# Banded attention inside a four-block kernel: strips loaded straight into the query and key tiles, the first group of heads loaded one stage early, four head groups folded by one product

## The chip, the cores and the metric

The kernel runs on one core of a Trainium2 chip. The metric is the device time of one execution in microseconds (us); lower is better. Engines are named as in the profile: PE is TensorE's matmul row and PEld its weight-load row, DVE is VectorE, ACT is ScalarE, POOL is GpSimd, SP is SyncE, which here only issues transfers. A name with a q behind it (SPq, ACTq, POOLq) is the queue that feeds the engine.

## The reference, cut to what matters

The input is x of shape (8, 512, 128): eight sequences of 512 tokens and 128 features. It passes through an expert layer, a state-space layer, the same expert layer, a routed expert layer ("ffn1"), banded attention, and the routed expert layer again. The change is in the attention and in the end of the ffn1 ahead of it.

```python
# attention: 16 heads of d = 8 features, blocks of C = 64 queries, a band 64 wide
qkv = (x @ Wqkv.T + bqkv).reshape(B, S, 3, H, d).transpose(2, 0, 3, 1, 4)
q, k, v = qkv[0], qkv[1], qkv[2]            # k and v padded by 32 on both sides
scores = einsum('bhncd,bhnld->bhncl', qc, kb) / sqrt(d)
scores = where(band, scores, -inf)          # band = (j >= c) & (j < c + 64)
o = einsum('bhncl,bhnld->bhncd', softmax(scores), vb)
out = o.transpose(0, 2, 1, 3).reshape(B, S, D) @ Wout.T + bout
```

## The kernel before

The program is a row of blocks, each with its own instruction list for every engine, and a barrier of all five engines between two of them: `front` (everything up to the first ffn1), `ffn1` with tag `_f` (in the profile: `_f1` in instruction lists), `attention` (tiles end in `_a`), and `ffn1` again with tag `_f1b`. `attention` is a generator: before its own block it hands out helpers (`opening`), with which the ffn1 block ahead prepares sequence 0, so that queries, keys and values are computed while the last expert tiles are still worked on.

**How attention is tiled.** A block is 32 queries against 96 keys (`QB`, `KW`), so a sequence has `NB` = 16 blocks. A group is 4 heads (`HG`), and a sequence has 4 groups, numbered n = 4s + g over the whole stage. A unit u is half of the blocks of one group (8 blocks); there are 8 units to a sequence and 64 in all. For one block one product gives the scores of all four heads of the group: the stationary operand is a block-diagonal query tile `qd` of 128 rows (head, copy, feature) by 128 columns (head, query), the moving operand 96 columns of the key tile `kT`. Queries and keys are split into a rounded part (`q_hi`, `k_hi`) and its rest (`q_lo`, `k_lo`), and the four copies of a head's 8 features are the four pairings of these parts.

**The way of a query.** ACT writes `q_hi`, DVE `q_lo`, both [128 features, 512 tokens]. SP stores each twice to `q_rows` in DRAM (`store_queries`), the same for keys (`store_keys`; for sequence 0 ACT issues these). `strips` reads a group's 128 rows back as `k_strips` and `q_strips` (256 KB each, two transfers per group). Then DVE copies the key strip into `kT` (`set_keys`, L1296) and ACT makes four copies of 32 rows each into the diagonal of `qd` (`set_queries`, L1287). There are three `qd`/`kT` pairs (`RQ`) and two strip pairs.

**The loop.** Step t of the PE loop is: scores of unit t+2 (L1311, 8 products), transposes of unit t's probabilities (`turn`, L1337, 8), the products with the values of unit t-1 (`weigh`, L1356, 8 products of two passes), and `gather` of unit t-2 (L1378, 8 products of two passes). `PLACES` adds, in the first four steps of a sequence, the next sequence's transposes, queries, keys and values and the last one's output projection (`project_pe`, L1265). The other engines follow in the same order: DVE masks and takes the maximum (L1320, L1325), POOL subtracts it (L1217), ACT takes the exponential (L1329), PE turns, ACT copies (L1344), PE weighs, DVE normalizes (L1363, L1367), POOL keeps each row's own head (`keep_own`, L1224).

**The fold.** After `weigh` a block's output has 128 rows (head, query) by 32 columns. `gather` multiplies it, as the stationary operand of 32 columns, with `fold` [128, 32], which sums the four quarters, and puts the result in rows 32g to 32g+31 of the bank `BZ`: one product for each block and each group. `BZ` is cleared once by DVE. When the eighth unit is in, ACT copies `BZ` to `oT` (`project_act`).

**Start of the stage.** After the barrier SP waits for the stores of sequence 0, loads groups 0 and 1 and stores and reloads the values. POOL clears the borders of all `kT` and all `qd` (L1228 to L1232), takes the norm of sequence 1 (`norm_root`), clears parts of the value tiles, adds the bias (L1212) and only then comes to the first subtraction. ACT's order is: queries 0, queries 1, exponential of unit 0, `norm_out(1)` (L104), exponential of unit 1. PE's third score product waits for group 1's tiles, and its next work after that is the transposes of sequence 1 (L114).

**End of the ffn1 ahead.** Its last part is a loop over J from 24 to 33 (`EJ` to `AJ`+1, `AJ` = 32), in which PE multiplies up (J) and down (J-2), with the opening's four pieces at J = 30, 31, 32, 33. POOL adds eight tiles of routed rows (L1679), and after the second it takes the norm of sequence 0, which waits for DVE's statistics (L74).

Of the kernel before, what the change touches and what calls it, by code (L numbers as in the profile page):

```python
# [984 lines left out]
def attention(nc, S, C, bank, K, a):  # L985
# [11 lines left out]
    with ExitStack() as ctx:  # L997
# [138 lines left out]

        def prep_act(eng, s, name):
# [6 lines left out]
            elif name in ("q", "k"):  # L1144
# [20 lines left out]
        yield dict(load_weights=load_weights, store_queries=store_queries, store_keys=store_keys, set_ones=set_ones, set_masks=set_masks, biases_pe=biases_pe, biases_dve=biases_dve,  # L1165
                   norm_stats=norm_stats, norm_root=norm_root, norm_out=norm_out, prep_pe=prep_pe, prep_act=prep_act, prep_dve=prep_dve)

        qd = [sb(f"qd{r}", [P, NB, HG, QB], F32R) for r in range(RQ)]
        kT = [sb(f"kT{r}", [P, PADDED], F32R) for r in range(RQ)]
        q_strips, k_strips = two("q_strips", [P, SEQ]), two("k_strips", [P, SEQ])  # L1170
# [4 lines left out]
        o1, oT = two("o1", [P, UB, GD]), sb("oT", [P, SEQ])  # L1175

        def strips(eng, s, g):
            n, heads = s * HG + g, slice(HG * g, HG * g + HG)
            if n >= 2:
                eng.wait_ge(q_set.sem, q_set.at(n - 2))  # L1180
                eng.wait_ge(k_set.sem, k_set.at(n - 2))
            eng.dma_start(k_strips[n % 2][:], k_rows[s, heads].rearrange("r c d t -> (r c d) t")).then_inc(strip_in[n % 2].sem, 16)
            eng.dma_start(q_strips[n % 2][:], q_rows[s, heads].rearrange("r c d t -> (r c d) t")).then_inc(strip_in[n % 2].sem, 16)
# [934 lines left out]
```

## Time and profile before

| | |
|---|---|
| median of 3 runs | 1942.12 us (1941.42 to 1945.63) |
| profiled execution, its own time | 1944.77 us |
| its span in the profile | 1943.0 us |
| mean granted PE clock | 0.966 of full speed |
| PE / PEld busy | 1770.6 us (91%) / 1520.2 us (78%) |
| DVE / ACT / POOL busy | 1223.9 / 1210.5 / 1200.7 us (62 to 63%) |
| ffn1 block ahead: first instruction after its barrier | 1142.0 us |
| attention block: released at / ends at | 1380.0 us / 1707.7 us |
| second ffn1 block ends | 1943.0 us |

The profile is one execution; times in it count from its span's start. Busy time of PE comes from modelled ends of matmuls, so the distance between starts of successive groups tells more than the length of one.

### The profile page before, as it was taken

What the parts mean: (1) busy time and instruction counts of PE and PEld (TensorE: products, weight loads), DVE (VectorE), ACT (ScalarE), POOL (GpSimd) and SP (SyncE); (2) the same over time, 40 slices, a digit from 0 to 9 for tenths busy, and PEclk for the clock granted to TensorE, in tenths of its full rate; (3) what the DMA queues carried; (4) which work ended last, traced back from release to release, by engine and by line L of the source; (5) the groups of instructions that cost most, each with busy time, mean ns of one, the idle gap of its engine ahead of it and who ended that gap; (6) DMA issues with size and microseconds to landing.
All of it is one profiled execution on the core that took longest, in us unless ns stands there. A gap on an engine that the chain in (4) does not pass through costs nothing. (4 is left out here: it accounts for less than half of the span.)

```text
span 1943.0 us, 35709 instructions
## 1 busy us (share of the span) xinstructions
PE 1770.6 (91%) x12117; PEld 1520.2 (78%) x12117; DVE 1223.9 (63%) x2897; ACT 1210.5 (62%) x2022; POOL 1200.7 (62%) x1195
## 2 busy tenths in 40 slices
PE   7999998999989989888789989999699999989998
PEld 6878776777777778766567878888599999978876
DVE  2358876767787677777886446433467666646433
ACT  3567777787687877778775554333477767543442
POOL 3148776776767757778896725465556555534664
PEclk9999998999999999999989989999799999989999
DMA  5023323222223323322231401112454444101113
GB/s 143 1 85 117 98 90 103 90 90 93 90 88 102 103 78 106 91 83 84 83 95 44 134 13 43 38 46 66 145 156 134 120 145 142 40 22 36 46 44 107
DMA packets 120638, 166.95 MB, mean 86 GB/s; under 512 B 13878, under 2 KB 55820, under 8 KB 120460
## 3 DMA queue, kind: packets, MB, share of 16 engines
q1 hardware_dynamic: 112716, 147.74, 25.3%
q0 software_dynamic: 7168, 15.87, 2.7%
q8 instruction: 101, 1.65, 0.3%
q10 hardware_dynamic: 576, 1.05, 0.2%
q14 instruction: 77, 0.63, 0.1%
HBM read 114.28 MB, written 50.33 MB: 85 GB/s over the span
## 5 line engine op out<-in xcount | busy, mean ns | idle before, releaser
L756 POOL TENSOR_TENSOR db<-du_m,bt 128x512 f32<-128x512 f32 x256 | 328.8, 1286 | 170.9 <-DVE bank L761 170.6
L761 DVE TENSOR_TENSOR_SCAN bank<-bank,db 128x512 f32<-128x512 f32 x256 | 312.6, 1221 | 27.2 <-ACT bank L746 27.0
L787 POOL TENSOR_TENSOR y_m<-y_m,ph 128x512 f32<-128x512 f32 x240 | 307.4, 1281 | 0.4 <-DVE ph L776 0.4
L746 ACT ACTIVATE bank<-dt_m,a_neg 128x512 f32<-128x512 f32 x256 | 176.2, 688 | 84.4 <-DVE ph L776 76.1
L776 DVE TENSOR_TENSOR ph<-bank,ct 128x512 f32<-128x512 f32 x240 | 165.9, 691 | 12.4 <-POOL y_m L787 4.4
L1217 POOL TENSOR_TENSOR s_a<-s_a,mx_a 128x768 f32<-128x768 f32 x64 | 94.1, 1470 | 89.1 <-DVE mx_a L1325 89.0
L1356 PE MATMUL bank<-vb_a,pT_a 96*128 96x64 f32 x1024 | 121.9, 272 | 0.2 <-DVE o_a L1367 0.2
L1356 PEld LDWEIGHTS bank<-vb_a,pT_a 96*128 96x128 f32 x1024 | 119.8, 192 | 0.3 <-DVE o_a L1367 0.3
L354 PEld LDWEIGHTS bank<-dn,hf2b 128*128 128x128 f32 x680 | 91.5, 196 | 14.3 <-DVE x_all L413 4.9
L354 PEld LDWEIGHTS bank<-dn,hf0b 128*128 128x128 f32 x688 | 91.5, 194 | 10.4 <-DVE x_all L413 2.8
L354 PEld LDWEIGHTS bank<-dn,hf1b 128*128 128x128 f32 x680 | 92.5, 198 | 8.1
L354 PEld LDWEIGHTS bank<-dn,hf2a 128*128 128x128 f32 x680 | 90.9, 195 | 8.5 <-DVE x_all L413 1.0
L354 PE MATMUL bank<-dn,hf2b 128*128 128x128 f32 x680 | 92.4, 280 | 5.5 <-DVE x_all L413 4.0
L354 PEld LDWEIGHTS bank<-dn,hf0a 128*128 128x128 f32 x688 | 90.5, 192 | 7.8 <-DVE x_all L413 0.3
L354 PEld LDWEIGHTS bank<-dn,hf1a 128*128 128x128 f32 x680 | 89.4, 192 | 7.5
L354 PE MATMUL bank<-dn,hf0b 128*128 128x128 f32 x688 | 92.2, 278 | 1.9 <-DVE x_all L413 1.9
L354 PE MATMUL bank<-dn,hf1b 128*128 128x128 f32 x680 | 92.8, 281 | 0.0
L354 PE MATMUL bank<-dn,hf2a 128*128 128x128 f32 x680 | 91.4, 278 | 0.5 <-DVE x_all L413 0.5
L354 PE MATMUL bank<-dn,hf0a 128*128 128x128 f32 x688 | 91.0, 275 | 0.0
L354 PE MATMUL bank<-dn,hf1a 128*128 128x128 f32 x680 | 89.8, 275 | 0.0
L1344 ACT COPY pT_a<-bank 96x512 f32<-96x512 f32 x128 | 68.1, 580 | 34.4 <-PE bank L1337 34.3
L1287 ACT CAST qd_a<-q_strips_a 32x512 fp32r<-32x512 f32 x128 | 78.7, 615 | 13.7 <-DMA q_strips_a<-q_rows 12.3
(453 smaller groups left out, 4952.0 us busy)
## 6 DMA issues: line engine op xcount, KB each, us to landing
bt<-bc_rows SPq DMA_DIRECT2D x128, 256.0 KB, 3.5
ct<-bc_rows SPq DMA_DIRECT2D x128, 256.0 KB, 3.4
sorted<-zero_row SPq DMA_DIRECT2D x64, 288.0 KB, 4.0
k_strips_a<-k_rows SPq DMA_DIRECT2D x32, 256.0 KB, 3.2
q_strips_a<-q_rows SPq DMA_DIRECT2D x32, 256.0 KB, 3.7
q_rows<-q_hi_a SPq DMA_DIRECT2D x16, 256.0 KB, 3.0
q_rows<-q_lo_a SPq DMA_DIRECT2D x16, 256.0 KB, 3.4
vb_a<-v_rows SPq DMA_DIRECT2D x16, 240.0 KB, 3.7
```

Of the source, the lines that this page charges most:

```text
L354: x = eng.matmul(Y.psum[:, t], hf[r][:, t], W["dn"][:, e, c, :], start=c == 0 and k == 0, stop=c == HC - 1 and k == NT - 1, skip_group_che ...
L746: eng.activation(DH[J % 2][:], dt[s % 2][:, j % NH, :], ACT.Exp, scale=a_neg[:, j % NH, j // NH:j // NH + 1]).then_inc(da_done.sem)
L756: eng.tensor_tensor(db[J % RD][:], du[s % 2][:, j % NH, :], bt[N % RB][:], ALU.mult).then_inc(db_done.sem)
L761: eng.tensor_tensor_scan(DH[J % 2][:], DH[J % 2][:], db[J % RD][:], 0.0, ALU.mult, ALU.add).then_inc(hs_done.sem)
L776: eng.tensor_tensor(out, DH[J % 2][:], ct[N % RB][:], ALU.mult).then_inc(ph_done.sem)
L787: eng.tensor_tensor(y[s % 2][:, j % NH, :], y[s % 2][:, j % NH, :], ph[J % RP][:], ALU.add).then_inc(ys_done.sem)
L1217: eng.tensor_tensor(X[:], X[:], M[:, :, None].to_broadcast([P, UB, KW]), ALU.subtract).then_inc(sub_done.sem)
L1287: x = eng.copy(qd[n % RQ][p, :, r, :], q_strips[n % 2][p, :].rearrange("p (b q) -> p b q", q=QB))
L1344: eng.copy(pT[u % 2][:, c * BB:(c + 1) * BB, :].rearrange("p b q -> p (b q)"), BT[c][0:KW, :]).then_inc(pT_done.sem)
L1356: x = eng.matmul(BO[:, at:at + 2 * GD], pT[u % 2][:, c * BB + j, :], vb[s % 2][:, b:NB + 1:NB - b, g * GD:(g + 1) * GD], start=True, stop= ...
```

## The change

1. `strips` loads a group's keys with one transfer into the middle of `kT` and its queries with four transfers of 32 partitions (64 KB each) into the diagonal of `qd`. `set_queries`, `set_keys`, the strip tiles and their counters are gone; PE waits for the transfers themselves, and SP waits for the scores of unit 2(n-3)+1 before it reloads a pair.
2. For that `qd` becomes [head, 512] instead of [block, head, query]. Queries are written in the order (query in block, block): `by_block` makes ACT and DVE write `q_hi` and `q_lo` with a step of 16 elements, and the scores' stationary operand reads block b as every 16th element, a step of 64 bytes. Before, its 128 columns lay side by side.
3. `o_all` [128, 16, 128] collects the outputs of all four groups of a sequence. `gather` runs twice for a sequence, after units 6 and 7, with the stationary operand 128 columns wide: 16 products for a sequence in place of 64. The clearing of `BZ` is gone.
4. In the ffn1 ahead the opening's pieces move: transposes to J = 29, queries to 30, keys to 31; statistics and norm one J earlier; DVE and ACT take queries before the J they stood behind. POOL clears pair 0 there (`clear_group`), SP stores `k_lo` and loads group 0 (`strips(0, 0)`), ACT stores `k_hi`. So group 0 is loaded before the barrier.

```diff
+        def by_block(tile, name):
+            return tile[:].rearrange("p (q b) -> p b q", b=NB) if name == "q" else tile[:].rearrange("p (b q) -> p b q", q=QB)
...
-                eng.activation(hi[:], X[:], ACT.Identity, bias=b_cols[:, col:col + 1]).then_inc(pa.sem)
+                eng.activation(by_block(hi, name), X[:].rearrange("p (b q) -> p b q", q=QB), ACT.Identity, bias=b_cols[:, col:col + 1]).then_inc(pa.sem)
...
+        def strips(eng, s, g):
+            n = s * HG + g
+            if g == 0:
+                eng.wait_ge(q_out.sem, q_out.at(s, "last"))
+                eng.wait_ge(k_out.sem, k_out.at(s, "last"))
+            q, ld = qd[n % RQ], strip_in[n % RQ]
+            if n >= RQ:
+                eng.wait_ge(sc_done.sem, sc_done.at(2 * (2 * (n - RQ) + 1) + 1))
+            else:
+                eng.wait_ge(zeroed.sem, zeroed.at(0, f"qd{n}"))
+            eng.dma_start(kT[n % RQ][:, PAD:PAD + SEQ].bitcast(F32), k_rows[s, HG * g:HG * g + HG].rearrange("r c d t -> (r c d) t")).then_inc(ld.sem, 16)
+            for h in range(HG):
+                eng.dma_start(q[32 * h:32 * h + 32, h, :].bitcast(F32), q_rows[s, HG * g + h].rearrange("c d t -> (c d) t")).then_inc(ld.sem, 16)
...
+        def clear_group(eng, r):
+            eng.memset(kT[r][:, 0:PAD].bitcast(F32), 0.0)
+            eng.memset(kT[r][:, PAD + SEQ:].bitcast(F32), 0.0)
+            eng.memset(qd[r][:].bitcast(F32), 0.0).then_inc(zeroed.sem)
...
-                eng.wait_ge(q_set.sem, q_set.at(n))
-                eng.wait_ge(k_set.sem, k_set.at(n))
+                eng.wait_ge(strip_in[n % RQ].sem, strip_in[n % RQ].at(n // RQ, f"q{HG - 1}"))
...
-                x = eng.matmul(BS[c][:, j * KW:(j + 1) * KW], qd[n % RQ][:, b, :, :].rearrange("p r q -> p (r q)"), kT[n % RQ][:, b * QB:b * QB + KW], start=True, stop=True)
+                x = eng.matmul(BS[c][:, j * KW:(j + 1) * KW], qd[n % RQ][:].rearrange("p h (q b) -> p (h q) b", b=NB)[:, :, b], kT[n % RQ][:, b * QB:b * QB + KW], start=True, stop=True)
...
+        def gather(eng, s, half):
+            if half == 0 and s >= 1:
                 eng.wait_ge(oc_done.sem, oc_done.at(s - 1))
-            eng.wait_ge(own_done.sem, own_done.at(u))
-            for j in range(UB):
-                b = half * UB + j
-                x = eng.matmul(BZ[32 * g:32 * g + 32, b * QB:(b + 1) * QB], o1[u % 2][:, j, :], fold[:], start=True, stop=True)
+            eng.wait_ge(own_done.sem, own_done.at(s * GU + GU - 2 + half))
+            for b in range(half * UB, (half + 1) * UB):
+                x = eng.matmul(BZ[:, b * QB:(b + 1) * QB], o_all[:, b, :], fold[:], start=True, stop=True)
             x.then_inc(ot_done.sem)
...
             if opening:
                 opening["store_queries"](eng, 0)
+                opening["store_low_keys"](eng, 0)
+                opening["strips"](eng, 0, 0)
...
-                if opening and J >= AJ - 2:
-                    opening["prep_pe"](eng, 0, ("T", "q", "k", "v")[J - AJ + 2])
+                if opening and J in (AJ - 3, AJ - 2, AJ - 1, AJ + 1):
+                    opening["prep_pe"](eng, 0, {AJ - 3: "T", AJ - 2: "q", AJ - 1: "k", AJ + 1: "v"}[J])
...
-                if opening and J == AJ - 4:
+                if opening and J == AJ - 5:
                     eng.wait_ge(added.sem, added.at(FINAL.index(0)))
                     opening["norm_stats"](eng, 0)
```

**PE, the steady loop** (from the products of a unit with the values to the scores of the next group; `o11_a` holds the outputs of one unit, `bank0` and `bank1` take scores, `bank2` and `bank3` transposes, `bank4` outputs, `bank5` is `BZ`). Before:

```order
L1356 MATMUL bank4<-vb0_a,pT0_a 128x64 [waits a_p_copied,a_out_dve]
L1356 MATMUL bank4<-vb0_a,pT0_a 128x64 x3
L1356 MATMUL bank4<-vb0_a,pT0_a 128x64 [waits a_p_copied]
L1356 MATMUL bank4<-vb0_a,pT0_a 128x64 x3
L1378 MATMUL bank5<-fold_a,o11_a 32x32 [waits a_own_kept]
L1378 MATMUL bank5<-fold_a,o11_a 32x32 x7
L1311 MATMUL bank0<-kT1_a,qd1_a 128x96 [waits a_masked,a_keys_set,a_queries_set]
L1311 MATMUL bank0<-kT1_a,qd1_a 128x96 x3
L1311 MATMUL bank1<-kT1_a,qd1_a 128x96 [waits a_masked]
L1311 MATMUL bank1<-kT1_a,qd1_a 128x96 x3
L1337 MATMUL bank2<-ident,s2_a 96x128 [waits a_p_copied,a_exp_done]
```

After, at the same place:

```order
L1360 MATMUL bank4<-vb0_a,pT0_a 128x64 [waits a_p_copied,a_out_dve]
L1360 MATMUL bank4<-vb0_a,pT0_a 128x64 x3
L1360 MATMUL bank4<-vb0_a,pT0_a 128x64 [waits a_p_copied]
L1360 MATMUL bank4<-vb0_a,pT0_a 128x64 x3
L1315 MATMUL bank0<-kT1_a,qd1_a 128x96 [waits a_masked,a_strips1_in]
L1315 MATMUL bank0<-kT1_a,qd1_a 128x96 x3
L1315 MATMUL bank1<-kT1_a,qd1_a 128x96 [waits a_masked]
L1315 MATMUL bank1<-kT1_a,qd1_a 128x96 x3
L1341 MATMUL bank2<-ident,s2_a 96x128 [waits a_p_copied,a_exp_done]
```

The fold has left the step and the wait for the copied tiles became a wait for the transfer. What stands for it now, once for each half of a sequence, here behind unit 6:

```order
L1360 MATMUL bank4<-vb0_a,pT1_a 128x64 [waits a_p_copied]
L1360 MATMUL bank4<-vb0_a,pT1_a 128x64 x3
L1379 MATMUL bank5<-fold_a,o_all_a 128x32 [waits a_own_kept]
L1379 MATMUL bank5<-fold_a,o_all_a 128x32 x7
L1315 MATMUL bank0<-kT2_a,qd2_a 128x96 [waits a_masked]
```

The product is 128 by 32 where it was 32 by 32.

**SP, from the end of the ffn1 ahead into attention** (`k_strips0_a` and `kT0_a` are targets of the key rows, `qd0_a` of the query rows). Before:

```order
L1046 DMA q_rows<-q_lo_a 16x8x512
L1046 DMA q_rows<-q_hi_a 16x8x512
L1046 DMA q_rows<-q_lo_a 16x8x512
L2066 UNCONDITIONAL_BRANCH
L1466 UNCONDITIONAL_BRANCH [waits barrier_Pool_Activation_PE_DVE_SP_release]
L1182 DMA k_strips0_a<-k_rows 128x512 [waits a_k_stored,a_q_stored]
L1183 DMA q_strips0_a<-q_rows 128x512
L1182 DMA k_strips1_a<-k_rows 128x512
L1183 DMA q_strips1_a<-q_rows 128x512
L1195 DMA v_rows<-xn_a 128x4x128 [waits a_prep_dve]
L1203 DMA vb0_a<-v_rows 32x15x128 [waits a_zeroed,a_v_stored]
```

After:

```order
L1044 DMA q_rows<-q_hi_a 16x8x512
L1044 DMA q_rows<-q_lo_a 16x8x512
L1054 DMA k_rows<-k_lo_a 16x8x512 [waits a_prep_dve]
L1054 DMA k_rows<-k_lo_a 16x8x512
L1183 DMA kT0_a<-k_rows 128x512 [waits a_zeroed,a_k_stored,a_q_stored]
L1185 DMA qd0_a<-q_rows 32x512 x4
L2059 UNCONDITIONAL_BRANCH
L1457 UNCONDITIONAL_BRANCH [waits barrier_Pool_Activation_PE_DVE_SP_release]
L1183 DMA kT1_a<-k_rows 128x512 [waits a_zeroed]
L1185 DMA qd1_a<-q_rows 32x512 x4
L1219 DMA v_rows<-xn_a 128x4x128 [waits a_prep_dve]
```

Group 0 is now loaded ahead of the block's end, and with it SP's wait for all eight stores of sequence 0; the low keys' stores came over from ACT's queue.

**POOL, the last adds of the ffn1 and the start of attention** (`yl` and `hT` hold the routed rows). Before:

```order
L1679 TENSOR_TENSOR x_all<-x_all,hT1_f1 128x512 [waits f1_rows3_loaded,f1_shared_acc]
L2066 UNCONDITIONAL_BRANCH
L1467 UNCONDITIONAL_BRANCH [waits barrier_Pool_Activation_PE_DVE_SP_gather]
L1228 MEMSET kT0_a 128x32
L1229 MEMSET kT0_a 128x32
L1228 MEMSET kT1_a 128x32
L1229 MEMSET kT1_a 128x32
L1228 MEMSET kT2_a 128x32
L1229 MEMSET kT2_a 128x32
L1232 MEMSET qd0_a 128x2048
L1232 MEMSET qd1_a 128x2048
L1232 MEMSET qd2_a 128x2048
```

After:

```order
L1190 MEMSET kT0_a 128x32
L1191 MEMSET kT0_a 128x32
L1192 MEMSET qd0_a 128x2048
L1674 TENSOR_TENSOR x_all<-x_all,yl0_f1 128x512 [waits f1_rows0_loaded,f1_shared_acc]
L1674 TENSOR_TENSOR x_all<-x_all,yl1_f1 128x512 [waits f1_rows1_loaded]
```

and, further on:

```order
L1674 TENSOR_TENSOR x_all<-x_all,hT1_f1 128x512 [waits f1_rows3_loaded,f1_shared_acc]
L2059 UNCONDITIONAL_BRANCH
L1458 UNCONDITIONAL_BRANCH [waits barrier_Pool_Activation_PE_DVE_SP_gather]
L1190 MEMSET kT1_a 128x32
L1191 MEMSET kT1_a 128x32
L1192 MEMSET qd1_a 128x2048
L1190 MEMSET kT2_a 128x32
L1191 MEMSET kT2_a 128x32
L1192 MEMSET qd2_a 128x2048
```

One of the three clearings of `qd` moved to a place ahead of the first add, the rest stayed behind the barrier.

## Rows read from the trace of the kernel before

**Rows 1.** The page, busy time and share of the span, by engine

```profile
PE 1770.6 (91%) x12117; PEld 1520.2 (78%) x12117; DVE 1223.9 (63%) x2897; ACT 1210.5 (62%) x2022; POOL 1200.7 (62%) x1195
```

**Rows 2.** Windows: stretch, length, busy by engine, PEclk, DMA share, GB/s

```profile
1373.00:1386.00 13.00, 1.04 (x8) 0.85 (x8) 3.23 (x12) 2.43 (x4) 5.74 (x9) 0.59 0.73 231
1386.00:1404.00 18.00, 15.32 (x70) 13.70 (x70) 11.30 (x15) 13.26 (x23) 9.94 (x16) 0.53 0.37 107
1500.00:1600.00 100.00, 98.80 (x1046) 92.45 (x1046) 69.98 (x173) 72.79 (x125) 58.41 (x61) 1.00 0.42 123
```

**Rows 3.** Timeline of the weight loads, one quiet step: start, us, engine, line

```profile
1504.52 0.58 PEld L1378 LDWEIGHTS bank<-fold_a,o_a 128*32 128x32 f32 x16
1505.14 0.97 PEld L1311 LDWEIGHTS bank<-kT_a,qd_a 128*128 128x128 f32 x8
1506.05 0.83 PEld L1337 LDWEIGHTS bank<-ident,s_a 128*96 128x96 f32 x8
1506.86 1.86 PEld L1356 LDWEIGHTS bank<-vb_a,pT_a 96*128 96x128 f32 x16
...
1508.80 0.58 PEld L1378 LDWEIGHTS bank<-fold_a,o_a 128*32 128x32 f32 x16
```

**Rows 4.** Groups in 1380 to 1720: count | busy, mean ns | idle before

```profile
L1287 ACT CAST qd_a<-q_strips_a 32x512 fp32r<-32x512 f32 x128 | 78.7, 615 | 13.7 <-DMA q_strips_a<-q_rows 12.3 <-POOL qd_a L1232 0.3
...
L1378 PEld LDWEIGHTS bank<-fold_a,o_a 128*32 128x32 f32 x1024 | 37.4, 113 | 9.5 <-issue 4.5 <-POOL o_a L1224 1.1
```

**Rows 5.** Timeline, two products with 512 moving columns back to back

```profile
1361.80 0.39 PE L119 MATMUL bank<-xT_lo_f,k_up_hi 128*128 128x512 f32 x1
1362.03 0.39 PE L120 MATMUL bank<-xT_hi_f,k_up_lo 128*128 128x512 f32 x1
```

**Rows 6.** Timeline over the barrier ahead of attention

```profile
1359.94 0.87 DVE L74 BATCH_NORM_STATS2 stats_a<-x_all 128x6 f32<-128x128 f32 x4
...
1368.06 2.50 POOL L1679 TENSOR_TENSOR x_all<-x_all,hT_f 128x512 f32<-128x512 f32 x2
...
1375.16 0.85 ACTq L1051 DMA_DIRECT2D k_rows<-k_lo_a  x1
1380.05 0.12 POOL L1228 MEMSET kT_a<- 128x32 f32 x1 [9.49 <-POOLq L2066]
...
1380.49 0.43 SPq L1183 DMA_DIRECT2D q_strips_a<-q_rows  x1
...
1383.53 2.50 ACT L1287 CAST qd_a<-q_strips_a 32x512 fp32r<-32x512 f32 x4 [12.28 <-DMA q_strips_a<-q_rows]
...
1386.08 1.78 PEld L1311 LDWEIGHTS bank<-kT_a,qd_a 128*128 128x128 f32 x8 [12.23 <-ACT qd_a L1287]
```

**Rows 7.** The source line of the ffn1's end: count, ns min/median/max, starts

```profile
L2066 POOLq DRAIN  x2: 10517/10840/11163, 1368.6 to 1932.3; - x2
```

**Rows 8.** Timeline of the stage's start

```profile
1380.68 5.57 POOL L1232 MEMSET qd_a<- 128x2048 f32 x3
...
1390.20 1.47 POOL L1217 TENSOR_TENSOR s_a<-s_a,mx_a 128x768 f32<-128x768 f32 x1
...
1392.45 1.63 ACT L104 ACTIVATE xn_a<-x_all,nm_a,rs_a 128x128 f32<-128x128 f32 x4
...
1394.27 0.71 PEld L114 LDWEIGHTS bank<-ident,xn_a 128*128 128x128 f32 x4
```

**Rows 9.** Timeline of the tail of attention

```profile
1701.31 0.58 PEld L1378 LDWEIGHTS bank<-fold_a,o_a 128*32 128x32 f32 x16
...
1703.01 0.86 PEld L1378 LDWEIGHTS bank<-fold_a,o_a 128*32 128x32 f32 x16 [1.12 <-POOL o_a L1224]
```

**Rows 10.** Timeline and transfers (x, KB, us to landing) at a sequence's first group

```profile
1520.24 0.97 PEld L1311 LDWEIGHTS bank<-kT_a,qd_a 128*128 128x128 f32 x8
...
1527.36 0.33 SPq L1182 DMA_DIRECT2D k_strips_a<-k_rows  x1
...
q_strips_a<-q_rows SPq DMA_DIRECT2D x3, 256.0 KB, 4.3
```

More of the change, by code:

```diff
@@ L1163, in prep_dve @@
                 eng.tensor_tensor(v_tok[:], X[:].rearrange("p (k d) -> p k d", d=D), b_all[:, 0:1, :].to_broadcast([P, NT, D]), ALU.add).then_inc(pd.sem)
[L1165 removed]
+        def strips(eng, s, g):
[15 more added lines that the diff above has]
+            eng.memset(qd[r][:].bitcast(F32), 0.0).then_inc(zeroed.sem)
+        with ExitStack() as ahead:
+            tiles = [[ahead.enter_context(nc.sbuf_tensor(f"{name}{r}_a", [P, *shape], F32R)) for name, shape in (("qd", (HG, SEQ)), ("kT", (PADDED,)))]
+                     for r in range(RQ)]
+        qd, kT = [t[0] for t in tiles], [t[1] for t in tiles]
+        yield dict(load_weights=load_weights, store_queries=store_queries, store_high_keys=store_high_keys, store_low_keys=store_low_keys, strips=strips, clear_group=clear_group, set_ones=set_ones, set_masks=set_masks, biases_pe=biases_pe, biases_dve=biases_dve,
                    norm_stats=norm_stats, norm_root=norm_root, norm_out=norm_out, prep_pe=prep_pe, prep_act=prep_act, prep_dve=prep_dve)
[L1168 to L1170 removed]
+        sb("groups", [P, RQ * (HG * SEQ + PADDED)])
         vb = two("vb", [KW, NB + 1, D])
@@ L1174, in attention @@
         pT, rc = two("pT", [KW, UB, P]), two("rc", [P, UB])
[L1175 to L1183, printed above, removed]
+        o_all, oT = sb("o_all", [P, NB, D]), sb("oT", [P, SEQ])
         def sync(eng):
@@ L1188, in sync @@
                     store_queries(eng, s)
-                    store_keys(eng, s)
-                eng.wait_ge(q_out.sem, q_out.at(s, "last"))
-                eng.wait_ge(k_out.sem, k_out.at(s, "last"))
-                strips(eng, s, 0)
+                    store_high_keys(eng, s)
+                    store_low_keys(eng, s)
+                    strips(eng, s, 0)
                 strips(eng, s, 1)
@@ L1219, in keep_own @@
         def keep_own(eng, u):
-            Z = o1[u % 2]
+            Z = o_of(u)
             if u == 0:
@@ L1359, in normalize @@
         def normalize(eng, u):
-            Z, R = o1[u % 2], rc[u % 2]
+            s, g, half = where(u)
+            R = rc[u % 2]
             O = BO[:].rearrange("p (b c) -> p b c", c=2 * GD)
@@ L2050, in dve @@
             for J in range(EJ, AJ + 2):
+                if opening and J in (AJ - 1, AJ):
+                    opening["prep_dve"](eng, 0, ("q", "k")[J - AJ + 1])
                 if J < AJ:
```

96 lines of the change are left out of this document (32 added, 64 removed).

## The prediction

> **What bounds the kernel now.** The page comes first: PE is busy 91% of the span and every other engine 62 to 63% [rows 1]. That is a mean over stages, so the windows come next. In the middle of attention PE is busy 98.8 of 100 us while DVE has 70, ACT 73 and POOL 58 [rows 2]. Work taken from DVE or ACT there shortens nothing by itself; work taken from PE does. Only the stage's start differs: from 1373 to 1386 PE does 1.0 us of work in 13, and in the 18 us behind it the granted clock is 0.53 of full speed, mostly the 1.2 GHz level, against 1.00 (2.4 GHz) later [rows 2]. There waits set the time. The timeline of one quiet step then gives PE's prices, read as distances between starts: fold 0.62 us (1504.52 to 1505.14), scores 0.91, transposes 0.81, values 1.94; the step is 4.28 us [rows 3].
>
> **Term 1, the copies.** ACT's 128 casts into `qd` (78.7 us) and DVE's 32 into `kT` go [rows 4]. In the steady loop they hide under PE: 73 and 70 busy in 100 us [rows 2]. I take zero. Without that cover (PE idle) they would be worth at most the waits that name them, 12 us, all at the start; term 3 counts that.
>
> **Term 2, the fold.** Before, each of 64 units folds in 0.62 us: 16 passes with a load of 32 columns, 0.039 us each. After, each of 16 halves has 16 passes with a load of 128 columns and 32 moving columns. The trace has no such pair. The nearest from below are the scores, eight loads of 128 columns in 0.91 us, 0.114 each; from above the values, 16 passes with 128-column loads in 1.94 us, 0.121 each, two passes per product as here [rows 3]. I take the second, which is also f32: 1.93 us for a half. A sequence then pays 3.86 instead of 4.96 us. Seven sequences: 7 x 1.10 = 7.7 us. In the last one six units' folds go (3.7 us), less 0.1 because the transposes alone (0.81) hardly cover DVE's normalization. Its tail now has two wide folds in a row, 3.9 us, where it took 1701.31 to about 1704.0, 2.7 us with a wait for POOL in it [rows 9]; that costs 1.2. Together 7.7 + 3.7 - 0.1 - 1.2 = **10.1 us**. With 0.114 for a pass it would be 12 us; a tail at the lower clock takes off up to 2, so 8 to 12.
>
> **Term 3, the start.** Two things have to be told apart: when the barrier opens, and what PE waits for behind it.
> The barrier opens at 1380.0. The last arrival is POOL's drain, which lasts 11.2 us from 1368.6 to 1379.8 [rows 7], 9.2 us beyond POOL's last add (1368.06 + 2.50) [rows 6]. The other engines were done by 1376.0 (end of ACT's last key store). So POOL's last add sets the barrier. The statistics that hold up POOL's norm, now at 1359.94 [rows 6], come one J earlier; a J is six products 0.23 us apart [rows 5] and eight passes of 0.11, some 2.3 us. POOL would be out at 1377.5. The clearing put ahead of its first add (a third of 5.57 us [rows 8], 1.9, plus two short ones) lies in its wait for the first reloaded rows; were that cover gone, it would cost 2 us. SP becomes the later one. The keys are also one J earlier, and the low keys' stores end near 1372.7. Before, the stores ended at 1376.0 and all had landed by 1380.1, so at most 4.1 us later; I take 3.5. The group's five issues, 0.4 us each, then end at 1378.2: one queue with five issues replaces two issues behind the barrier. **The barrier opens 1.8 us earlier.**
> Behind it PE now waits for the strips (12.3 us on ACT's line) and ACT's four copies, 2.5 us, until 1386.08 [rows 6]. A group lands 3.4 us from its first issue (1380.10 to 1383.53); with three issues more, PE starts at about 1380.9, 5.2 us earlier. But PE cannot keep that. Its third score product no longer waits for DVE's key cast; its next work, sequence 1's transposes (1394.27), waits for ACT's normalization (1392.45), which stands behind the first exponential and so behind POOL's first subtraction (1390.20) [rows 8]. That comes 10.15 us after the barrier; with one clearing of three gone, 8.3. So this chain runs 1.8 + 1.9 = **3.7 us** earlier. The rise of the clock came behind continuous work that starts with those transposes, so I let it move with them. Bounds: 1.9 (the barrier does not move) and 5.2 (all of PE's earlier start is kept).
>
> **Term 4, the strided loads.** The scores' stationary operand now steps 64 bytes from column to column, 512 times. No operand in this trace is read so, so the cost is bounded from both sides. From below zero: PE's moving side takes 512 columns of four bytes in 0.23 us [rows 5], 2.2 columns a nanosecond, while a load takes 128 in 0.114 us, 1.1 a nanosecond. The load path asks for half the rate that a read path is seen to give, and so has room. From above, one load takes twice its time, 0.107 us more for the 128 columns net of a pass's overhead: 512 x 0.107 = 55 us. A gain is excluded, since fewer useful bytes are never read faster. I take zero, because rate and room point there, and keep 55 as an end. The strided writes of `q_hi` and `q_lo` are 16 in all at 0.7 us; doubled, they lie under PE, save two at the start, at most 1 us in the bounds of term 3.
> The Trainium skill speaks against this choice. "Advanced Engine Details and Errata", section SBUF Cachelines, says that SBUF has 16-byte lines, that at least two hits on a line are needed to absorb the latency, and that a new line for each access carries a penalty. Here each column lies on a line of its own. No run here shows it yet; by that rule the sum ends above the old time if the penalty is a doubling, by rows alone it ends below.
>
> **The sum.** 10.1 + 3.7 = 13.8 us. The profiled execution took 1944.8 us, so 1931.0 for a like one; its time is 2.7 above the median of the runs, so 1942.1 - 13.8 = **1928.3** for the median.
>
> **Rivals.**
> Stride dear (0.18): every load of `qd` takes 0.22 us instead of 0.11. The scores' 0.91 becomes 1.76 and nothing hides it, since PE is the bound. 1928.3 + 55 = 1983, slower by 2%. It decides against the change from 13.8/512 = 27 ns a load on. For it speaks that no row excludes it; against it the room above.
> Stride partly dear (0.09): 5 to 35 ns a load, 3 to 18 us: 1931 to 1946.
> Strips late (0.05): a sequence's first group is loaded when its key stores have landed. Before, SP issues it 7.1 us after the scores at 1520.24 [rows 10]. PE needs it four steps after those scores, 4 x 3.66 us plus two preparations of 0.9, 16.4 us. Issues take 2.0 and landing 4.3 [rows 10]: 13.4. The margin is 3 us; if quarter-height transfers land at 7.3 us or later, PE stalls seven times. At 9 us that is 12 us, and the result about 1940. Groups 1 to 3 have over 10 us.
> Only the fold (inside the forecast): the barrier doesn't move or the clock rises as late as before, 1930 to 1932.
> Not as announced (0.03): something unseen takes over, such as DVE's output writes into rows of 128, which could lengthen a chain of 0.9 us that PE's 1.72 covers.
>
> **How the numbers follow.** The forecast case has 0.65 and its own range is 1921 to 1933: 12 + 5.2 and a little more off at one end, 8 + 1.9 at the other. The range for 8 in 10 must take in the partly dear loads and the late strips: 1920 to 1950 holds 0.65 + 0.09 + 0.05 and a part of the rest. The doubling stays outside. A change under 0.2% (4 us) cannot be told from none. Faster by more: 0.65, half of the partly dear case and half of the late strips, 0.71. Within: 0.06. Slower: 0.18, and the upper parts of the small cases, 0.23.
>
> **What would show it.** In the timeline of a quiet step: scores still 0.91 us from their start to the transposes' (right) or 1.3 and more (stride). The fold's line with 512 passes instead of 1024, 16 of them in 1.8 to 1.95 us. A step of 3.66 us without the fold. The barrier near 1378, with SP and no longer POOL last; PE's first score product near 1381; sequence 1's transposes near 1390.5 with POOL's subtraction ahead in the chain. PE's idle time on the score line in front of a sequence's first group near zero. The prediction is wrong if the loads stretch, if that idle time is there, or if the barrier stays at 1380.

## The result, and the profile after

The changed kernel takes 2132.3 us (median of 4 runs, 2128.8 to 2136.1), beside 1943.9 us for the kernel before on the same chip: ratio 1.098, 95% interval 1.095 to 1.100. It is slower by 188 us. The forecast of 1928.3 us was wrong, and its range did not hold the time. The rival that came nearest, "stride dear" with 1983 us, has the sign and is 149 us short.

The page of the changed kernel, with the slices of PE and of the granted clock:

```profile
span 2132.1 us, 33964 instructions
PE 1967.2 (92%) x11349; PEld 1713.6 (80%) x11349; DVE 1217.9 (57%) x2864; ACT 1145.5 (54%) x1894; POOL 1196.0 (56%) x1195
...
PE   7999998999999999878998999799999999989998
PEclk9999999999999999999999999865555555559999
```

Against [rows 1] PE is busy 197 us longer, though it has fewer products; the copies' work on ACT is gone (1145.5 us) and buys nothing. The last row is the one to look at: the ten slices from 1386 to 1919 us read 5 or 6, and all but the end of them is attention. The same stretches as in [rows 2] (length, busy time by engine, PEclk, DMA share, GB/s):

```profile
1373.00:1386.00 13.00, 5.03 (x22) 4.86 (x22) 5.23 (x16) 1.28 (x1) 7.67 (x18) 0.52 0.47 149
1386.00:1404.00 18.00, 15.04 (x81) 13.15 (x81) 8.48 (x13) 10.24 (x17) 7.63 (x7) 0.68 0.61 165
...
1500.00:1600.00 100.00, 100.00 (x478) 94.66 (x478) 39.92 (x87) 29.02 (x46) 30.22 (x31) 0.55 0.27 80
```

In the middle of attention PE never idles, yet it gets 478 products done in 100 us instead of 1046. Part of that is the fold, which has left the step: 48 products a step before, 32 now. The rest is slowness, and the granted clock is 0.55 instead of 1.00: nearly always the 1.2 GHz level. The fall can be seen in the timeline of the weight loads:

```profile
1402.51 1.86 PEld L1360 LDWEIGHTS bank<-vb_a,pT_a 96*128 96x128 f32 x16
1404.30 1.83 PEld L1315 LDWEIGHTS bank<-kT_a,qd_a 128*128 128x128 f32 x8
1406.04 0.99 PEld L1137 LDWEIGHTS bank<-w_v_a,xT_a 128*128 128x128 f32 x8
1406.94 0.89 PEld L1341 LDWEIGHTS bank<-ident,s_a 128*96 128x96 f32 x8
1407.82 1.87 PEld L1360 LDWEIGHTS bank<-vb_a,pT_a 96*128 96x128 f32 x16
1409.60 1.83 PEld L1315 LDWEIGHTS bank<-kT_a,qd_a 128*128 128x128 f32 x8
1411.38 1.52 PEld L1341 LDWEIGHTS bank<-ident,s_a 128*96 128x96 f32 x8
1412.90 3.54 PEld L1360 LDWEIGHTS bank<-vb_a,pT_a 96*128 96x128 f32 x16
1416.32 1.85 PEld L1315 LDWEIGHTS bank<-kT_a,qd_a 128*128 128x128 f32 x8
1418.12 1.51 PEld L1341 LDWEIGHTS bank<-ident,s_a 128*96 128x96 f32 x8
1419.65 3.53 PEld L1360 LDWEIGHTS bank<-vb_a,pT_a 96*128 96x128 f32 x16
1423.06 1.85 PEld L1315 LDWEIGHTS bank<-kT_a,qd_a 128*128 128x128 f32 x8
```

Two things stand in it. First, while the clock is still full, eight score loads (L1315) take 1.74 us from 1404.30 to 1406.04, where [rows 3] have 0.91: 0.22 us a load instead of 0.11. The step doubles the load. Second, at 1411.4 the clock falls: transposes (L1341) and values (L1360) take 1.5 and 3.4 us instead of 0.88 and 1.79. The strided scores themselves take 1.80 us after the fall, hardly longer than before it. A step at full clock would be 1.74 + 0.88 + 1.79 = 4.4 us; at the lower clock it is 6.74 (1416.32 to 1423.06), against 4.28 in [rows 3], where the fold is in it too. PE had no idle time ahead of the fall.

The start, as in [rows 6, 8]:

```profile
1363.67 2.53 POOL L1674 TENSOR_TENSOR x_all<-x_all,hT_f 128x512 f32<-128x512 f32 x2
1375.85 1.82 SPq L1185 DMA_DIRECT2D qd_a<-q_rows  x4
1378.08 0.12 POOL L1190 MEMSET kT_a<- 128x32 f32 x1 [11.88 <-POOLq L2059]
1379.41 3.68 PEld L1315 LDWEIGHTS bank<-kT_a,qd_a 128*128 128x128 f32 x16 [9.32 <-DMA qd_a<-q_rows]
1385.84 4.31 POOL L1241 TENSOR_TENSOR s_a<-s_a,mx_a 128x768 f32<-128x768 f32 x3
1389.77 0.72 PEld L114 LDWEIGHTS bank<-ident,xn_a 128*128 128x128 f32 x4 [3.12 <-ACT xn_a L104]
```

The barrier opens at 1378.1 (forecast 1378.2), PE's first score product starts at 1379.4 (1380.9) and sequence 1's transposes at 1389.8 (1390.5), 4.5 us earlier than before. This term came nearly as forecast and is lost in the rest.

For the experiments I need a length of attention that does not depend on the stages around it. I take the first start on the scores' line to the last start on the output projection's line, in the one profiled execution of each run. Changed kernel (count, ns min/median/max, first and last start):

```profile
L1315 PEld LDWEIGHTS bank<-kT_a,qd_a x512: 291/314/337, 1379.4 to 1867.6; 128*128 128x128 f32 x171
L1285 PEld LDWEIGHTS bank<-w_o_a,oT_a x64: 288/333/338, 1460.3 to 1896.4; 128*128 128x128 f32 x64
```

That is 1896.4 - 1379.4 = 517.0 us. The kernel before has 1706.1 - 1386.1 = 320.0.

### The profile page after: what moved, and what is told of

It reads as the page before. It is cut to its first block and busy times, and to the rows that moved or that the text cites. A ratio compares the mean times of both kernels' runs of the same rounds, so it can differ in the third digit from the quotient of the medians.

```text
span 2132.1 us, 33964 instructions
## 1 busy us (share of the span) xinstructions
PE 1967.2 (92%) x11349; PEld 1713.6 (80%) x11349; DVE 1217.9 (57%) x2864; ACT 1145.5 (54%) x1894; POOL 1196.0 (56%) x1195
## 3 DMA queue, kind: packets, MB, share of 16 engines
q8 instruction: 95, 1.56, 0.3%
## 5 line engine op out<-in xcount | busy, mean ns | idle before, releaser
L1360 PEld LDWEIGHTS bank<-vb_a,pT_a 96*128 96x128 f32 x1024 | 205.6, 306 | 1.7 <-DVE o_all_a L1372 0.9
L1360 PE MATMUL bank<-vb_a,pT_a 96*128 96x64 f32 x1024 | 203.8, 385 | 0.8 <-DVE o_all_a L1372 0.8
L1348 ACT COPY pT_a<-bank 96x512 f32<-96x512 f32 x128 | 74.4, 583 | 194.3 <-PE bank L1341 193.6
L1248 POOL TENSOR_TENSOR o_all_a<-o_all_a,own_a 128x256 f32<-128x256 f32 x64 | 46.4, 725 | 186.7 <-DVE o_all_a L1372 186.7
L1315 PE MATMUL bank<-kT_a,qd_a 128*128 128x96 f32 x512 | 124.9, 412 | 10.7 <-DMA qd_a<-q_rows 10.7
L1368 DVE RECIPROCAL rc_a<-bank 128x8 f32<-128x8 f32 x64 | 13.3, 207 | 203.2 <-PE bank L1360 203.2
L1315 PEld LDWEIGHTS bank<-kT_a,qd_a 128*128 128x128 f32 x512 | 118.4, 315 | 11.4 <-DMA qd_a<-q_rows 11.0
L1341 PE MATMUL bank<-ident,s_a 128*96 128x128 f32 x512 | 120.4, 414 | 0.0
L1324 DVE SCALAR_TENSOR_TENSOR s_a<-bank,band_a 128x384 f32<-128x384 f32 x128 | 69.5, 553 | 65.2 <-PE bank L1315 65.2
L1341 PEld LDWEIGHTS bank<-ident,s_a 128*96 128x96 f32 x512 | 95.8, 195 | 12.5 <-issue 8.2
```

The costliest lines, as they stand in the source:

```text
L1315: x = eng.matmul(BS[c][:, j * KW:(j + 1) * KW], qd[n % RQ][:].rearrange("p h (q b) -> p (h q) b", b=NB)[:, :, b], kT[n % RQ][:, b * QB:b * ...
L1324: eng.scalar_tensor_tensor(sc[u % 4][:, c * BB:(c + 1) * BB, :], BS[c][:, 0:BB * KW].rearrange("p (b k) -> p b k", k=KW), scale, band[:, N ...
L1341: x = eng.transpose(BT[c][0:KW, j * P:(j + 1) * P], sc[u % 4][:, c * BB + j, :], C["ident"][:])
L1348: eng.copy(pT[u % 2][:, c * BB:(c + 1) * BB, :].rearrange("p b q -> p (b q)"), BT[c][0:KW, :]).then_inc(pT_done.sem)
L1360: x = eng.matmul(BO[:, at:at + 2 * GD], pT[u % 2][:, c * BB + j, :], vb[s % 2][:, b:NB + 1:NB - b, g * GD:(g + 1) * GD], start=True, stop= ...
```

## The experiments

**Theory A:** each strided load takes twice its time; PE then spends more of its time loading and less multiplying; the clock answers to what the array does and falls to its lower level, which slows everything else. **Rival B:** the stride costs its 55 us and the wide fold takes the clock. **Rival C:** the stride is not at fault. **Rival E:** the strided reads as such, and not the thin work, lower the clock. Work is called thin where few moving columns go through the array for each load of 128 columns, and dense where many do. D is set out in the expectation of e2, F and G in that of e5.

Chips differ (the kernel before takes 1941.4, 1955.3 and 1962.5 us beside the three groups of runs), so ratios to the kernel before on the same chip count. The attention lengths are from one execution each and from different chips: the same kernel gives 306.9 and 306.8 on two of them (e6, e12), but where the clock is low, two executions of one kernel lie up to 27 us apart (e9; 16 in e1, 15 in e7). Differences of attention under 20 us between such runs are read from the ratios.

| run | stationary columns | fold | ratio (95%) | clock 1500:1600 | attention, us |
|---|---|---|---|---|---|
| changed kernel | 64 bytes apart | wide, 32 moving | 1.098 (1.095 to 1.100) | 0.55 | 517.0 |
| e1 | 64 bytes | narrow, old start and copies | 1.079 (1.073 to 1.084) | 0.67 | 477.3 |
| e2 | contiguous | wide, 32 | 1.005 (1.003 to 1.008) | 0.82 | 335.5 |
| e3 | 16 bytes | wide, 32 | 1.095 (1.092 to 1.099) | 0.57 | 519.5 |
| e4 | contiguous + thin second product | wide, 32 | 1.119 (1.115 to 1.124) | 0.57 | 553.3 |
| e5 | contiguous | narrow | 0.999 (0.997 to 1.002) | 1.00 | 322.6 |
| e6 | contiguous | wide, 64 moving | 0.991 (0.989 to 0.993) | 1.00 | 306.9 |
| e7 | 64 bytes | narrow | 1.074 (1.070 to 1.078) | 0.76 | 457.8 |
| e8 | 64 bytes + dense fillers | wide, 32 | 1.091 (1.088 to 1.094) | 0.67 | 501.2 |
| e9 | contiguous + dense second product | wide, 32 | 1.026 (1.019 to 1.033) | 0.95 | 367.5 |
| e10 | 8 bytes | wide, 64 | 0.990 (0.986 to 0.993) | 1.00 | 304.3 |
| e11 | 64 bytes | wide, 64 | 1.076 (1.071 to 1.082) | 0.67 | 475.7 |
| e12 | as e6 | wide, 64 | 0.991 (0.987 to 0.994) | 0.98 | 306.8 |

### e1: the stride alone

```
-        qd = [sb(f"qd{r}", [P, NB, HG, QB], F32R) ...
+        qd = [sb(f"qd{r}", [P, HG, SEQ], F32R) ...
-   x = eng.copy(qd[n % RQ][p, :, r, :], q_strips[n % 2][p, :].rearrange("p (b q) -> p b q", q=QB))
+   x = eng.copy(qd[n % RQ][p, r, :], q_strips[n % 2][p, :])
-   qd[n % RQ][:, b, :, :].rearrange("p r q -> p (r q)")
+   qd[n % RQ][:].rearrange("p h (q b) -> p (h q) b", b=NB)[:, :, b]
```

> The kernel before with one edit: queries are written query by query, the copies into the query tiles are contiguous, and the scores' stationary operand steps 64 bytes from column to column. The copies, the narrow fold and the stage's start stay as they were. Theory A (each strided load doubles, and the thinner work then loses the clock): a score group of eight takes 1.75 to 1.85 us instead of 0.91, the granted clock in 1500:1600 is near 0.55 instead of 1.00, and the time is 2120 to 2160 us. Rival B (the stride costs only its 55 us, and the wide fold takes the clock): the same score group, but a granted clock of 1.00 and 1995 to 2005 us. Rival C (the stride is not at fault at all): 0.91 us and 1944 us.

Measured 2094.6 us. The stride alone makes the kernel slow: C falls, and B too, since the clock is 0.67 with the old fold. Theory A's 2120 to 2160 us and its clock near 0.55 are both missed, the time by 25 us on the low side; something else in the change also takes from the clock.

### e2 and e3: contiguous, and 16 bytes apart

```
+        QE = 1      # e3: 4
-        ("qd", (HG, SEQ))
+        ("qd", (NB // QE, HG, QB * QE))
-   qd[n % RQ][:].rearrange("p h (q b) -> p (h q) b", b=NB)[:, :, b]
+   qd[n % RQ][:, b // QE].rearrange("p h (q e) -> p (h q) e", e=QE)[:, :, b % QE]
```

> The changed kernel with one edit: queries are kept block by block, so that a block's 32 queries stand side by side for each head, and the four transfers of a group fetch pieces of 128 bytes. Strips still go straight to the tiles, the fold is wide, the start is the new one. Theory A: scores 0.91 us, granted clock 1.00 in 1500:1600, and the forecast's 1928 us (1920 to 1935). Rival B: scores 0.91 us but the clock near 0.55, over 2050 us. Rival D (pieces of 128 bytes land late and PE waits at each sequence's first group): idle time on the score line in front of it, 1935 to 1960 us.

> The changed kernel with a step of 16 bytes instead of 64 between the columns of the stationary operand (four blocks interleaved), pieces of 512 bytes in the transfers, and four instructions instead of one for each strided write of the queries. By the rule of the Trainium skill, page Advanced Engine Details and Errata, section SBUF Cachelines (lines of 16 bytes, one column on each line here too), a load should cost as much as at 64 bytes: scores 1.75 us and 2130 us. If instead a load is slowed by the distance, or by banks met again at 64 bytes, scores are 0.91 us and the time is that of the contiguous variant plus up to 6 us for the added instructions at the start. The sum by rows: 0.22 us for a load if the cost is the same for each step above 4 bytes, 0.11 if not.

e2 takes back 181.5 of attention's 197 us, so the step of the stationary operand is at the root of nearly all. But it reaches 1951.0 us, not 1928, and neither A nor B foretold that. Rival D's 1935 to 1960 us holds the time, but not for D's reason: PE's waits for strips are 11.6 us in all and lie at the start, so D falls. The windows show what is left:

```profile
1504.00:1536.00 32.00, 31.72 (x282) 30.97 (x281) 22.63 (x59) 16.87 (x29) 20.05 (x22) 1.00 0.68 164
1536.00:1560.00 24.00, 24.00 (x103) 21.64 (x103) 8.31 (x15) 5.76 (x9) 5.61 (x5) 0.50 0.39 110
```

24 us at the lower clock, with PE busy without a gap. The timeline of the loads says what stood ahead of the fall:

```profile
1532.24 1.86 PEld L1362 LDWEIGHTS bank<-vb_a,pT_a 96*128 96x128 f32 x16
1534.03 1.87 PEld L1381 LDWEIGHTS bank<-fold_a,o_all_a 128*128 128x128 f32 x16
1535.82 1.56 PEld L1317 LDWEIGHTS bank<-kT_a,qd_a 128*128 128x128 f32 x8
...
1549.21 1.83 PEld L1317 LDWEIGHTS bank<-kT_a,qd_a 128*128 128x128 f32 x8
1550.91 1.83 PEld L1287 LDWEIGHTS bank<-w_o_a,oT_a 128*128 128x128 f32 x8
```

The wide fold (L1381): 16 loads of 128 columns with 32 moving columns each. The scores behind it are already slow (1.56 instead of 0.97). So there seems to be a second cause, of the same kind as the first; e5 and e6 test it. The last two lines give eight contiguous score loads at the lower clock: 1.70 us (1549.21 to 1550.91).

e3 lands where the line rule puts it, 2129.6 us against the expected 2130. Its loads are no faster than at 64 bytes, as its timeline shows before the clock falls:

```profile
1405.15 1.86 PEld L1372 LDWEIGHTS bank<-vb_a,pT_a 96*128 96x128 f32 x16
1406.94 1.95 PEld L1327 LDWEIGHTS bank<-kT_a,qd_a 128*128 128x128 f32 x8
1408.79 0.99 PEld L1137 LDWEIGHTS bank<-w_v_a,xT_a 128*128 128x128 f32 x8
```

Eight loads take 1.85 us (1406.94 to 1408.79), 0.23 each, at full clock: the values ahead of them take 1.79.

### e4 and e9: thin work and dense work, both contiguous

Each score product is followed by a second product of contiguous operands. In e4 it moves 16 columns, in e9 128; the loads are the same.

```
+   # e4
+   x = eng.matmul(BS[c][:, at:at + 16], kT[n % RQ][:, 0:P], kT[n % RQ][:, b * QB:b * QB + 16], ...)
+   # e9
+   x = eng.matmul(BS[c][:, BB * KW:BB * KW + P], kT[n % RQ][:, 0:P], kT[n % RQ][:, P:2 * P], ...)
```

> The contiguous variant, with a second product behind each score product: a contiguous load of 128 columns and only 16 moving columns, written to unused columns of the scores' bank. PE then needs as long for scores as with strided loads, but reads nothing with a step. Theory A (the clock is lost because PE spends its time on loads with little array work between them): scores near 1.8 us, clock near 0.55 in 1500:1600, 2080 to 2150 us. Rival E (the strided reads as such lose the clock): the clock stays 1.00 and the time is 1928 + 512 x 0.114 = 1986 us.

> The kernel of e4 with one edit: the second product behind each score product moves 128 columns instead of 16. Loads and their number are the same, and a pass is still bounded by its load of 0.114 us, so PE's time should hardly change at a given clock (0.12 us a product at most, by the values' passes: 2 to 4 us more in all). Theory A (the clock follows the array's work): the clock stays 1.00, and the time falls from 2173 to 1951 + 58, less what the wide fold's dips cost, 1986 to 2015 us. Rival (the clock follows the loads, or the number of products, or the power of the reads): 2170 us or more again.

e4 has no strided read at all, its clock is 0.57, and it is slower than the changed kernel: 2173.5 us. Rival E with its 1986 us and a clock of 1.00 falls: the clock is lost without any stride. That strided reads take something of their own besides is not excluded, but nothing asks for it: e7, strided, keeps more clock (0.76) than e4, contiguous. The time misses A's 2080 to 2150 us by 23 on the high side. One reason is in its timeline: e4 copies the strided loads' time only at full clock:

```profile
1470.60 0.19 PEld L1317 LDWEIGHTS bank<-kT_a,qd_a 128*128 128x128 f32 x1
...
1472.42 1.09 PEld L1346 LDWEIGHTS bank<-ident,s_a 128*96 128x96 f32 x8
...
1476.94 0.33 PEld L1317 LDWEIGHTS bank<-kT_a,qd_a 128*128 128x128 f32 x1
...
1480.42 1.51 PEld L1346 LDWEIGHTS bank<-ident,s_a 128*96 128x96 f32 x8
```

A unit's scores with their added products take 1.82 us at full clock (1470.60 to 1472.42), like eight strided loads, but 3.48 us at the lower one (1476.94 to 1480.42), where eight strided loads take 1.80.

e9 does eight times the multiplying in the added products and takes 186 us less of attention. First e4, then e9:

```profile
1500.00:1600.00 100.00, 100.00 (x511) 95.39 (x511) 34.24 (x78) 26.35 (x43) 28.62 (x30) 0.57 0.26 65
```

```profile
1500.00:1600.00 100.00, 100.00 (x843) 97.74 (x842) 58.32 (x137) 41.68 (x70) 47.77 (x50) 0.95 0.50 122
```

PE is busy 100 of 100 us in both. Beside the chip only the added products' moving operand and its place in the bank differ, and with them the clock: 0.57 against 0.95. With the ratio of e9, 1942.1 x 1.026 = 1992 us, inside A's 1986 to 2015; its two executions are 27 us apart (2001.1, the profiled one, and 2028.2), which is small beside the step from a ratio of 1.119 to 1.026. The clock was to stay at 1.00 and is 0.95. This is the pair that carries theory A; the ends of the stage in the two:

```profile
L1287 PEld LDWEIGHTS bank<-w_o_a,oT_a x64: 191/333/334, 1461.7 to 1930.7; 128*128 128x128 f32 x64
```

```profile
L1287 PEld LDWEIGHTS bank<-w_o_a,oT_a x64: 192/333/338, 1454.0 to 1756.2; 128*128 128x128 f32 x64
```

### e5, e6 and e12: the fold without the stride

e5 puts the narrow fold back into e2. e6 keeps the wide one and lets each product move 64 columns; e12 is e6 again.

```
-   x = eng.matmul(BZ[:, b * QB:(b + 1) * QB], o_all[:, b, :], fold[:], ...)
+   w = 2 if b < NB - 1 else 1
+   x = eng.matmul(BZ[:, b * QB:(b + w) * QB], o_all[:, b, :], fold[:, None, :].to_broadcast([P, w, QB]), ...)
```

> The contiguous variant (e2) with the old fold as well: each unit's eight blocks folded at once, 32 columns loaded for each pass. What is left of the change is that strips go straight to the tiles and that the stage starts earlier. Theory F (the wide fold pulls the clock down in parts of a sequence, which cost the contiguous variant 23 us against the forecast's 1928): the granted clock is 1.00 in 1500:1600 and 1600:1700, and the time is before less what the start gives, 1942 - 3 = 1938 to 1940 us. Rival G (the clock dips come from the transfers of 128 bytes or from the missing copies on ACT and DVE): the clock stays near 0.83 and the time is 1950 us or more.

> The contiguous variant (e2) with the wide fold, but each product moves 64 columns instead of 32 (the fold matrix read twice; the second half lands on columns that the next product overwrites). The loads are the same, so PE's time for a fold should be nearly the same, 1.95 us by the values' passes of 0.121 us with 64 moving columns, and the array does twice the work in it. Theory F with array work as the cause: the dips behind the folds go or get shorter, and the time is 1929 (all gone) to 1942 us. Rival (the dip comes with any run of 128-column loads, whatever moves): 1951 us again.

> The kernel of e6 once more, beside e10 on one chip. Expected the same ratio to the kernel before as in e6, 0.991 (0.989 to 0.993), and the same time as e10 within 2 us.

In e5 and e6 the clock holds: 1.00 in 1500:1600. G, which put e2's dips down to small transfers or missing copies, falls, since e5 has both. e6's loads of the fold are those of e2; it needs 28.6 us less for attention, and the only difference in the kernel is that more columns move:

```profile
1500.00:1600.00 100.00, 99.12 (x856) 95.27 (x856) 67.83 (x162) 51.56 (x91) 57.09 (x59) 1.00 0.59 145
```

e6 and e12 give 0.991 each: 1942.1 x 0.991 = 1924 us, 5 us under the low end of what I expected. This version beats both kernels, by 0.9% over the kernel before. e5's 0.999 has an interval from 0.997 to 1.002. It holds my expected 0.998 as well as no gain, so it does not tell the start's 4 us from nothing.

### e7, e8 and e11: the stride kept

e7 is the changed kernel with the narrow fold. e8 adds two dense products behind each four score products, e11 moves 64 columns in the fold.

```
+   # e8
+   for j in range(2):
+       x = eng.matmul(BS[c][:, BB * KW:BB * KW + P], kT[n % RQ][:, j * P:(j + 1) * P], kT[n % RQ][:, P:2 * P], ...)
```

> The changed kernel with the old fold: strided loads and narrow fold, strips straight to the tiles, new start. If wide fold and strided loads both take from the clock, this is the first experiment's 2094.5 us less the start's 3 us, 2085 to 2100; if the wide fold makes no difference beside the stride, 2130 to 2140 us.

> The changed kernel with its strided loads, and two products more behind each four score products, four a unit: a contiguous load of 128 columns and 128 moving columns, written to unused columns of the scores' bank. PE gets 64 x 4 x 0.114 = 29 us more to do at full clock. Theory A (the clock follows the array's work): the clock comes back for much of the stage, and although more is done the time falls, to 2012 us if the clock is always back (1928 + 55 + 29) and to 2050 to 2100 if it is back in parts. Rival (strided reads or something else holds the clock down): 2132 + 50, above 2170 us, since at the lower clock each filler costs twice.

> The changed kernel with its stride of 64 bytes, only the fold moves 64 columns instead of 32. If the fold's thin work matters beside the stride as it does without it, part of the 59 us between strided loads with wide fold (attention 517 us) and with narrow fold (458 us) comes back: attention 480 to 500 us, 2095 to 2115 us. If beside the stride the scores alone keep the clock down, 2125 to 2135 us.

e7: attention is 59 us shorter than in the changed kernel (46 us by the ratios, 1.098 and 1.074), although the narrow fold is the dearer one at full clock. Its ratio makes 2086 us of 1942.1, inside the expected 2085 to 2100. e11: 41 us shorter by moving more columns (43 by the ratios); at 475.7 us it lies a little below the expected 480 to 500. e8: 256 products more, some 29 us of work at full clock, and attention is 16 us shorter (501.2 against 517.0; 14 by the ratios, whose intervals do not overlap), not 50 us longer as the rival had it. My 2012 to 2100 us for it was too hopeful against the measured 2131.4: the clock came back to 0.67, not to 1.00.

### e10: 8 bytes apart

The kernel of e6 with QE = 2: two blocks interleaved.

> The kernel of e6 (contiguous queries, fold with 64 moving columns) with a step of 8 bytes between the stationary operand's columns: two blocks interleaved, transfers in pieces of 256 bytes. With lines of 16 bytes two columns share a line, and by the Trainium skill, page Advanced Engine Details and Errata, section SBUF Cachelines, two hits suffice: scores 0.91 us as in e6. If a load is slowed for every step above 4 bytes, scores take about 1.75 us and the time is 1936 + 55 and what the clock loses, over 1990 us. Whether larger pieces save anything against e6: the strips land one to two us earlier at the start, so 0 to 2 us.

Ratio 0.990 beside 0.991 for e12 on the same chip: no difference that these runs can tell. The loads in its timeline:

```profile
1511.08 1.87 PEld L1392 LDWEIGHTS bank<-fold_a,o_all_a 128*128 128x128 f32 x16
1512.87 1.02 PEld L1327 LDWEIGHTS bank<-kT_a,qd_a 128*128 128x128 f32 x8
1513.82 0.30 PEld L1130 LDWEIGHTS bank<-xT_a,w_q_a 128*128 128x128 f32 x2
```

Eight loads take 0.95 us (1512.87 to 1513.82), 0.119 each, against 0.114 contiguous in [rows 3]. So the doubling begins between 8 and 16 bytes of step. The Trainium skill's page "Advanced Engine Details and Errata", section SBUF Cachelines, says it with lines of 16 bytes and two hits wanted on each: by that rule full rate is kept up to 8 bytes and lost from 16 on. The traces agree at 4, 8, 16 and 64 bytes; the penalty, for which the page has no figure, is 0.10 to 0.12 us for 128 columns here.

## Why the prediction was wrong

**Term 4 is the step that failed**, twice over.

Its choice was wrong. I took zero, on the ground that a load asks for 1.1 columns a nanosecond where the moving side is seen to read 2.2, "and so has room". A read rate seen on contiguous data says nothing about columns in separate lines. The upper end, twice the load, is what came: 0.22 us, and eight loads in 1.74 us where the rival said 1.76. (The 0.107 us that it added for a load is worked out from none of the rows shown; measured it is 0.83 / 8 = 0.104.) I had the rule that spoke against the choice beside it, and gave rows that could not decide the question more weight than it.

Its bound was wrong too, and that is the larger error. I called 55 us the end from above. It priced the loads and held the clock at 1.00, as [rows 2] show it. Measured at full clock the loads cost 64 x (1.74 - 0.91) = 53 us. The stage is 197 us longer. Against e6, which keeps the clock but for the start and short dips, the changed kernel has 517.0 - 306.9 = 210 us more: 53 for the loads at full clock, and a rest of 157 for the clock. The steps bear the rest out: 6.74 less 4.4 us, 64 times, would be 150. The split holds for this order alone. At the lower clock a strided group costs only 0.10 us more than a contiguous one (1.80 against e2's 1.70), 6 us in 64; the stride's real price is that it loses the clock. The lower level was in my rows, 0.53 in 1386:1404, but I read it as a matter of waits: PE idle, then slow. Here PE is busy throughout. That thin work by itself can take the clock from a busy PE is shown by e4 against e9.

**Term 2, the fold,** was priced right for its time and wrong for the whole. A wide half takes 1.79 us (e2: 1534.03 to 1535.82), not 1.93, so the lower bound from the scores' rows, 16 x 0.114 = 1.82, was the better one. The values also take 1.79 us (1402.51 to 1404.30 above) and not the 1.94 of [rows 3], where the narrow fold stands behind them; the saving of fold and seam together is e5's 322.6 less e6's 306.9, 15.7 us, against 10.1 forecast. But in the form of the change, with 32 moving columns, the wide fold lowers the clock in part of a sequence: e2 needs 28.6 us more than e6 for attention. So the term would not have been a gain of 10 us without the stride either: the contiguous variant with this fold ends at 1.005 (1.003 to 1.008), slightly slower than the kernel before.

**Term 1** was right: nothing for the copies (e5, which has none, is at 0.999). No wait of PE names strips later than the start, and "strips late" did not come, with pieces of 128 bytes (e2) either.

**Term 3** was right in its places and 0.8 us short in size: 4.5 us instead of 3.7 at sequence 1's transposes. SP is now the last at the barrier: its five issues end at 1377.7, POOL's drain at 1375.5. The low keys' stores, for whose 1372.7 the prediction shows no working, ended at 1372.4.

**The two causes do not simply add.** The stride costs attention 181.5 us beside the thin wide fold (517.0 - 335.5), 169 beside the dense one (475.7 - 306.8) and 135 beside the narrow one (457.8 - 322.6). By the ratios of whole times it is 179, 166 and 145 us, each good to some 6 to 13 us (an estimate from their intervals), so only the first and the last clearly differ. No single price stands for the stride. That it depends on how near the rest of the work is to losing the clock fits this, but is argued and not shown.

What is left open: how the start's gain shows in the whole time (e5), why the strided scores take hardly longer after the clock's fall than before it (1.80 against 1.74 us), and whether strided reads take from the clock beyond their longer time.

## What to carry to other kernels

Where TensorE bounds a stage, ask of a change not only what it adds to TensorE's time but how much multiplying stands in that time: loads of 128 columns with few moving columns are thin, and a stage that is full can lose its clock without one idle gap. Where full rate matters, let the columns of a stationary operand lie at most 8 bytes apart, by interleaving few blocks (here two) if whole rows must land by DMA. And when a bound is worked out from durations, say at which granted clock, and price the other level as a case of its own.

## What the hardware showed that I had not expected

- A full TensorE at the lower clock: 100.00 of 100 us busy and a granted clock of 0.55 (changed kernel), 0.57 (e4). The Trainium skill's page "TensorE: Matmul & The Clock Gate", Part 1, section "The HAM clock gate", describes a monitor that sets the clock by how busy PE has been. Busy time as the profile counts it is not that: e4 and e9 both have 100 of 100 us, and clocks of 0.57 and 0.95.
- More work in less time: e9 over e4 (367.5 against 553.3 us of attention), e6 over e2 (306.9 against 335.5), e8 over the changed kernel (501.2 against 517.0).
- The time of a load depends on the step between its columns: 0.114 us contiguous, 0.119 at 8 bytes, 0.23 at 16, 0.22 at 64. The section "LDWEIGHTS (loading the stationary operand)" of the Trainium skill's page "TensorE: Matmul & The Clock Gate" gives it by the number of columns alone; at 16 and 64 bytes that does not hold here.
- A strided group of eight scores takes 1.74 us at full clock and 1.80 us at the lower one (1416.32 to 1418.12), while a contiguous group needs 0.91 [rows 3] and 1.70 (e2, 1549.21 to 1550.91). The step costs 0.83 us a group at full clock and 0.10 at the lower one.
- POOL's drain at the barrier did not shrink when its last add came 4.4 us earlier: 11.3 us in the changed kernel, 11.2 in [rows 7].

```profile
L2059 POOLq DRAIN  x2: 10517/10891/11265, 1364.2 to 2121.3; - x2
L2059 SPq DRAIN  x2: 7/64/122, 1377.7 to 2127.1; - x2
```
